# A hybrid layer on one Trainium2 core: the first gate and up unit of the second shared product is issued among the expert tiles

## What is computed

```python
x = x + attn_a(layernorm(x))     # a state-space block, 8 groups of 16 heads, with a convolution in front
x = x + ffn(layernorm(x))        # mixture of experts
x = x + layernorm(x) @ (weight * block_mask).T
x = x + ffn(layernorm(x))        # the same mixture of experts, the same weights

def ffn(x2):                     # 1024 tokens, 512 wide
    shared = (silu(x2 @ Sg.T) * (x2 @ Su.T)) @ Sd.T           # 512 hidden columns, every token
    top2   = the two largest of softmax(x2 @ gate_w.T), scaled to a sum of 1     # 16 experts
    moe    = sum over the two experts e of weight_e * (silu(x2 @ G_e.T) * (x2 @ U_e.T)) @ D_e   # 128 hidden columns
    return moe + shared
```

## Time and profile before

| | us |
|---|---|
| median of 3 runs | 2001.85 |
| lowest and highest of them | 2001.73, 2005.4 |
| the profiled execution: its own time | 1995.66 |
| its span, first to last instruction | 1993.9 |
| PE busy in the span | 1960.6 |
| DVE busy | 1467.4 |
| ACT busy | 1191.9 |
| POOL busy | 1032.7 |

### The profile page before, as it was taken

The page is one execution under the profiler, slowest core; times in us unless marked ns, Lnnn a source line. Parts: engine busy times, 40 slices in busy tenths (PEclk is TensorE's granted clock), DMA queues, the critical chain, the costliest instruction groups (busy, mean ns, idle before and its releaser), DMA issues.

```text
span 1993.9 us, 38125 instructions
## 1 busy us (share of the span) xinstructions
PE 1960.6 (98%) x11776; PEld 1632.7 (82%) x11776; DVE 1467.4 (74%) x2764; ACT 1191.9 (60%) x2602; POOL 1032.7 (52%) x907
## 2 busy tenths in 40 slices
PE   5999999999999999999999999999999999999999
PEld 4888888888888888888888888888888878877887
DVE  8998499849975997599759966996698673167315
ACT  4795388538853884388448744974496444534442
POOL 1596059616951694179417932792289315440433
PEclk8999999999999999999999999999999999999999
DMA  3552145114511351234123413341243139951996
GB/s 107 168 168 58 42 121 168 57 40 124 163 53 57 120 155 48 73 111 152 44 88 109 140 44 93 113 131 43 92 130 113 54 107 327 378 156 48 313 386 198
DMA packets 143909, 253.92 MB, mean 127 GB/s; under 512 B 21448, under 2 KB 37832, under 8 KB 143696
## 3 DMA queue, kind: packets, MB, share of 16 engines
q1 hardware_dynamic: 134848, 231.35, 36.8%
q0 software_dynamic: 7520, 16.80, 2.8%
q10 hardware_dynamic: 1328, 3.15, 0.4%
HBM read 233.38 MB, written 25.69 MB: 130 GB/s over the span
## 4 chain that ended last, share of the span: by engine, by line
PE 91%; DVE 5%; issue 2%; ACT 1%; DMA 1%; DVEq 0%; ACTq 0%; SPq 0%; POOL 0%; POOLq 0%
PE bank L1683 61%; PE bank L1802 7%; PE bank L1992 6%; PE bank L1816 6%; PE bank L1756 4%; PE bank L2004 3%; PE bank L1784 2%; DVE Y L1283 1%; PE bank L1979 1%; PE bank L1691 1%; DVE spare L1380 1%; PE bank L1775 1%; PE bank L1823 1%; DVE Y L1292 1%; DMA cv<-xn_dram,toks 0%
## 5 line engine op out<-in xcount | busy, mean ns | idle before, releaser
L1683 PE MATMUL bank<-xh,wh 128*128 128x512 f32 x1288 | 523.9, 407 | 7.4 <-POOL wl L720 4.0
L1683 PE MATMUL bank<-xh,wl 128*128 128x512 f32 x1288 | 504.9, 392 | 0.0
L1683 PE MATMUL bank<-xl,wh 128*128 128x512 f32 x1288 | 502.8, 390 | 0.0
L720 POOL TENSOR_TENSOR wl<-raw,wh 128x512 fp32r<-128x512 f32 x144 | 192.8, 1344 | 456.7 <-ACT wh L870 456.7
L1283 DVE SCALAR_TENSOR_TENSOR Y<-bank,cpar,Y 128x511 f32<-128x511 f32 (+2 forms) x384 | 286.8, 747 | 23.3 <-ACT Y L914 13.9
L1683 PEld LDWEIGHTS bank<-xh,wh 128*128 128x128 f32 x1288 | 243.0, 189 | 57.2 <-POOL wl L720 4.9
L1683 PEld LDWEIGHTS bank<-xh,wl 128*128 128x128 f32 x1288 | 242.3, 188 | 54.4
L1683 PEld LDWEIGHTS bank<-xl,wh 128*128 128x128 f32 x1288 | 243.4, 189 | 45.8 <-issue 0.5
L737 POOL TENSOR_TENSOR Y<-Y,gt 128x512 f32<-128x512 f32 x128 | 184.1, 1439 | 94.5 <-DVE gt L1337 92.7
L1345 DVE TENSOR_TENSOR al<-Y,ah 128x512 fp32r<-128x512 f32 x128 | 95.8, 749 | 184.3 <-ACT ah L972 184.3
L1683 PE MATMUL bank<-wh,ah 128*128 128x512 f32 x544 | 213.6, 393 | 0.5
(11 more groups left out here) (231 smaller groups left out, 4028.2 us busy)
## 6 DMA issues: line engine op xcount, KB each, us to landing
mem<-c_rows SPq DMA_DIRECT2D x128, 256.0 KB, 3.9
mem<-wffn_d SPq DMA_DIRECT2D x62, 512.0 KB, 6.2
E<-e_rows SPq DMA_DIRECT2D x256, 96.0 KB, 3.5
raw<-wconv_d SPq DMA_DIRECT2D x80, 256.0 KB, 3.0
cv<-c_rows SPq DMA_DIRECT2D x64, 256.0 KB, 4.0
spare<-c_rows SPq DMA_DIRECT2D x64, 256.0 KB, 4.1
raw<-wgate_d SPq DMA_DIRECT2D x64, 256.0 KB, 2.7
raw<-wout_d SPq DMA_DIRECT2D x64, 256.0 KB, 2.7
```

What stands on the lines that cost most here:

```text
L720: inc(pool.tensor_tensor(wl[:, W_SLOT[p], :], raw[:, R_SLOT[p], :], wh[:, W_SLOT[p], :], ALU.subtract), w_lo)
L1683: got = mm(out, l, r, start=first and n == 0, stop=last and n == 2)
```

## The change

In both runs the gate and up matmuls of unit 0 of the second shared product are issued behind the down product of tile 15, in iteration k = 16 of PE's tile loop, ahead of gate and up of tile 17. They go to the banks 4 and 7 in place of 0 and 2. ACT takes the tanh at its k = 16 and makes the high part at k = 17; DVE multiplies behind the hidden rows of tile 16 and makes the low part behind those of tile 17. No work is added or taken out. PE waits for the first shared product's last down add (and in run 0 for the mask, which used bank 4) in place of the end of the tiles.

```diff
+        GU0_AT = 16
+
+        def ffn_banks(i, j):
+            return (4, 7) if i % 2 and j == 0 else (j % 2, 2 + j % 2)
...
-                inc(nc.scalar.activation(gt[:, j % 2, :], bank[j % 2][:, :], ACT.Tanh, scale=0.5), f_th)
+                inc(nc.scalar.activation(gt[:, j % 2, :], bank[ffn_banks(i, j)[0]][:, :], ACT.Tanh, scale=0.5), f_th)
...
                     if 20 <= k <= 21:
                         w_part(second, k - 16)
-                for j in range(4):
+                    if k == GU0_AT:
+                        hidden_tanh(second, 0)
+                    if k == GU0_AT + 1:
+                        hidden_hi(second, 0)
+                for j in range(1, 4):
                     hidden_tanh(second, j)
                     hidden_hi(second, j)
...
-                    inc(STT(gt[:, j % 2, :], gt[:, j % 2, :], 1.0, bank[j % 2][:, :], ALU.add,
+                    inc(STT(gt[:, j % 2, :], gt[:, j % 2, :], 1.0, bank[ffn_banks(i, j)[0]][:, :], ALU.add,
                             ALU.mult), f_hg)
...
-                    inc(TTn(gt[:, j % 2, :], gt[:, j % 2, :], bank[2 + j % 2][:, :], ALU.mult), f_h)
+                    inc(TTn(gt[:, j % 2, :], gt[:, j % 2, :], bank[ffn_banks(i, j)[1]][:, :], ALU.mult), f_h)
...
                 for tau in range(TILES):
                     t_hidden(tau)
+                    if tau == GU0_AT:
+                        hidden_gate(second, 0)
+                        hidden_up(second, 0)
+                    if tau == GU0_AT + 1:
+                        hidden_lo(second, 0)
...
-                hidden(second, 0)
                 combine(0)
                 hidden(second, 1)
...
-                    base, name = ((0, g_mm), (2, u_mm))[n]
+                    name = (g_mm, u_mm)[n]
                     if b == 0:
                         now(pe, f_lo, i, 3 * a + n + 1)
-                    if j >= 2:
+                    if i % 2 and j == 0:
+                        now(pe, dn_acc, i - 1, TT)
+                        if run == 0:
+                            pe.wait_ge(mask_on, 1)
+                    elif j >= 2:
                         now(pe, f_h, i, j - 1)
                     elif i % 2:
                         pe.wait_ge(tx_ok, job(run, TILES))
...
-                        last = three(bank[base + j % 2][:, :], xh[:, kt, b * SEQ:(b + 1) * SEQ],
+                        last = three(bank[ffn_banks(i, j)[n]][:, :], xh[:, kt, b * SEQ:(b + 1) * SEQ],
...
                     if k:
                         t_down(k - 1)
+                    if k == GU0_AT:
+                        gate_up(second, 0, 0, 0)
+                        gate_up(second, 0, 0, 1)
...
-                for what, a, b in FFN_ORDER:
+                for what, a, b in FFN_ORDER[1:]:
```

## The result

The changed kernel takes 2006.76 us (median of 20 runs, 2003.91 to 2009.4) against 2003.06 us (20 runs) for the kernel before beside it: a ratio of 1.0019, with a 95% interval of 1.0013 to 1.0026. That is 3.7 us slower, where 7.2 was forecast. Its own profiled execution took 2004.34 us, with a span of 2002.6, and stands 8.7 us over the profiled execution of before. The two profiles differ by more than twice the medians; most of this study is about why. The profiled execution of before, at 1995.66 us, also lies under all 20 runs of its kernel here, of which the lowest is 1999.43.

A forecast was written before the change was run, and what follows sets the result against it. PE, with 91% of the last chain, was taken to bound the tile loop, and gathers and DVE the tail behind it. Run 0's +3.8 and run 1's +3.4 gave +7.2 us on 2001.85: 2009.0 us, range 2005 to 2014.5.

The forecast's parts named there:

- within 0.2%: Outcome class for the whole kernel: time within 0.2% (4 us) of the kernel before, chance 0.11.
- The move on PE: Tile loop: the unit's 24 matmuls put off the loop's end and first gather by 5.45 us in each run.
- Restarts: PE's changes between tile and shared matmuls in the loop: 0.15 us a run, at most 0.24 each, twice a run.
- What the pause gives back: Tiles behind k = 16: late down weights catch up during the unit, returning 1.5 us in run 0, 1.4 in run 1.
- a unit that is free in the loop: Tile loop: with transfers at 374 GB/s near the 435 GB/s ceiling, the unit would cost nothing; the sum kept 5.45 us.
- The tail of run 0: Behind run 0's loop: DVE's string moves with the loop's end, less its 0.34 us wait for PE; entered as -0.3 us.
- The tail of run 1: Behind run 1's loop: DVE ends 32.7 us behind the loop instead of 33.5, so 0.8 us come back.
- New waits of PE: Tail of run 0: PE waits 1.7 us before unit 3 and 0.9 before down 1, both covered by 3 us.
- The tail follows PE: Rival on both tails: PE sets their end, so the move cancels and relief remains: -2.6 us, 1999.2; chance 0.06.
- the loop follows the transfers: Rival on the tile loop: weights set its pace, the unit is hidden, only tails gain: -1.1 us, 2000.7; chance 0.05.
- No relief: Rival on the tile loop: late tiles stay late, or a new PE wait counts: +10.1 us, 2012.0; chance 0.25.
- the one on the base: Whole kernel: the profiled execution lies 6.2 us under the median of 2001.85, taken as the base for 2009.0.

The follow-up runs named there:

- c_before: The kernel before, unchanged, run again on the first chip: 1995.42 us, ratio 1.0.
- c_after: The changed kernel, unchanged, run again on the first chip: 2003.91 us, ratio 1.0046 to the kernel before.
- h_late: The kernel before with five POOL instructions put ahead of each tail's first gather, third chip: 2007.88 us, ratio 1.0014.
- n_after: The changed kernel without the 16 gathers and the combines of each tail, second chip: 1993.2 us, ratio 0.9933 to the kernel before.
- d_before: The kernel before, unchanged, run again on the third chip: 2005.48 us, ratio 0.9998.
- d_after: The changed kernel, unchanged, run again on the third chip: 2008.23 us, ratio 1.0017 to the kernel before.
- f_spread: The kernel before with the two weight loads of iteration 16 moved to 12 and 20, their splits to 18 and 26: 2022.65 us, ratio 1.0084.
- n_before: The kernel before without the 16 gathers and the combines of each tail, second chip: 1994.84 us, ratio 0.9948 to the kernel before.
- g_early: The kernel before with the first of the two weight loads issued at iteration 9 instead of 16: 2004.39 us, ratio 0.9997.
- s_before: The kernel before with the two weight loads at iteration 16 cut to 16 of 512 columns: 2005.57 us, ratio 0.9994.

## Why the prediction was right, and which term was mis-sized

The direction and the range held, the range with some luck. 2006.76 us lies under the 2008.0 that the terms alone give as their lowest; it is inside because 3 us were added for the spread of the runs. The difference of 3.7 us lies outside the forecast's own 6.2 to 8.5, and at 0.19% it fell on the side of "within 0.2%", which had a chance of 0.11 (the interval reaches to 0.26%). On the first chip the sum can be held against c_before and c_after directly.

**The move on PE** (forecast 5.45 us a run): 5.48 measured. **Restarts** (0.15): none seen. **What the pause gives back** (1.5 and 1.4): the loops grew by 3.97 and 3.87 us, which looks like 1.5 and 1.6. In run 0 that is right: c_before loses 1.6 us behind tile 15 and c_after 0.1. In run 1 it is luck: c_before loses 0.1 us behind tile 15 and 1.4 ahead of it, where the unit can't help, and c_after happens to lose nothing there. This is the term that was mis-sized. Over the twelve loops of the six profiles with the unit behind the tiles, the loss behind tile 15 is 0.1 to 2.4 us and 1.0 on average; with the unit at 16 it is 0.0 to 0.1. So the pause gives back about 1.0 us a run and not 1.5. The prediction took it from one profile, and it had read only run 0's first sixteen iterations, which lose nothing in its window, while those of run 1 lose 1.4 us in the same profile. The cause was named too narrowly as well: the two loads at SP's iteration 16 make tile 19 late, but the loops lose about as much elsewhere with them shrunk or moved.

The Trainium skill (Perfetto Trace Analysis, section Roofline) says that the 16 DMA engines bound a single core at about 435 GB/s. The 374 GB/s of the earlier trace rows stay under it. The consequence that the prediction drew from it, a unit that is free in the loop, didn't come: the unit cost the loops 3.9 us of its 5.5.

**The tail of run 0** (-0.3): -0.1 between c_before and c_after. **The tail of run 1** (-0.8): -0.8. **New waits of PE**: in run 0 1.7 us ahead of unit 3 and 0.9 ahead of down 1 were forecast, and 1.74 and 1.40 came (1.29 and 1.26 in c_after); for run 1 none was named, and 1.16 and 0.86 came. They were covered, as forecast, but by less than the 3 us given: PE waits 1.8 us for the first normed row. The prediction had also read its start wrongly. The earlier trace rows is the second set of transposes; the first is

```profile
1786.35 1.09 PE L1691 MATMUL bank<-ident,cv 128*128 128x128 f32 x8 [0.16 <-DVE cv L1189]
```

so in the kernel before PE and DVE end this tail 0.16 us apart, and not 0.81. These terms make 7.6 us of c_after's 7.7 us in span, but 0.7 us of it comes from ahead of the first loop, where the change does nothing, and the 1.4 us of run 1's early tiles count the other way. With 1.0 us of relief a run the sum would be 11.0 - 2.0 - 0.9 = 8.1 us (an estimate from these profiles) against 8.9 measured by the medians; the forecast was 7.2. Counted from the loop's end, the first gather of run 0 starts 4.2 to 4.7 us behind it in the four profiles of a moved unit with gathers, against 3.6 without the move (h_late aside) and in every run 1; I hadn't foreseen this, and no run isolates its cause.

**Rivals.** "The tail follows PE" and "the loop follows the transfers" would have had c_after at or below c_before; it is 8.9 us above. "No relief" gave +10.1, and the loops show relief; but 8.9 lies between it and the forecast. n_after shows the first rival's mechanism where its condition is made true.

**The step that was off most** is the one on the base: "it lies 6.2 us under the median of 2001.85, which I take as the base". I put the distance between the profiled execution and the median down as a constant that both kernels carry. It isn't one. The kernel before is 11.2 us longer in span on the third chip than on the first (2004.5 against 1993.3), and 11.0 of that is its two tails: 5.9 and 5.1 us. The changed kernel is 4.3 us longer, 1.9 of it in the tails and 2.3 in the loop of run 1, whose early tiles lose 2.2 us more. So the forecast's +7.2 stands on a chip like the one whose profile was read (+8.9 measured), and on the others the kernel before loses in its tails most of what it had ahead. The chip of the first comparison wasn't profiled for the kernel before beside its 20 runs; that it is of the second kind is argued, not shown. For it speak its medians, 2003.06 and 2006.76, and a mark in the profiles: in the first profile of before and in all four of the first chip the profile gives the time to landing of the down weights, 5.1 to 5.6 us (5.4 in the earlier trace rows); in the eight of the other two chips, and in that of the changed kernel beside the 20 runs, it gives none. d_before's row:

```profile
mem<-wffn_d SPq DMA_DIRECT2D x42, 256.0 KB
```

Each chip was used in one session only, so chip and session aren't parted either.

Why the changed kernel loses less is shown as far as this: the waits without a releaser fall from 18.2 us to 1.2. That its tails run one unit fewer, as I expected for d_after, isn't the reason by itself: h_late runs all four units beside its gathers, only with the gathers 4.5 us later, and has 4.3 us of such waits. It may be where the gathers stand against units 2 and 3; no run tests that. No kernel here with the whole computation in it beat the kernel before by more than its interval.

## What to carry to other kernels

Before work is moved off a busy tail, ask what starts at the end of the stage that it moves into: here each 5.5 us unit ahead of the last tile put off sixteen gathers by as much, less about 1 us of late tiles, and the idle time that it left behind was time in which the tail waited anyway. A profiled execution some microseconds under the median is a warning that what stretches the others isn't in the rows; find it before its absence is priced. And before a load or a split is moved along a queue, read what is queued behind its waits, as f_spread shows with 5 us a run. A term of 1 or 2 us needs several profiles: the loops of one program differ by that much.

## What the runs showed that I had not expected

The same program takes 1995 us on one chip and 2005 to 2007 on two others, at a granted clock of 0.995 to 0.996 on both kinds (d_before, c_before), and the difference is in two stretches of about 40 us. In them the results of the gate and up matmuls reach ACT and DVE late, after 1.5 to 5.7 us of idle time each for units 2 and 3, while POOL's indirect gathers run. Without the gathers (n_before, second chip) the tails are 30.1 and 33.4 us and no such wait is there. In d_before the last gather is issued by 1987.2 and the late tanh starts at 1989.11; in run 0 they are at 1778.4 and 1780.36. g_early (run 0), s_before and f_spread (run 1) have the same late tanh, and in all five it starts 1.5 to 2.0 us behind the end of the last gather's instruction.

The signal is late and not the matmuls. PE in d_before, tail of run 1:

```profile
1983.90 0.39 PE L1683 MATMUL bank<-xh,wl 128*128 128x512 f32 x1
1984.13 0.39 PE L1683 MATMUL bank<-wh,ah 128*128 128x512 f32 x1
...
1986.91 0.40 PE L1683 MATMUL bank<-wl,ah 128*128 128x512 f32 x1 [0.35 <-issue]
1987.63 0.48 PE L1683 MATMUL bank<-wh,al 128*128 128x512 f32 x1 [0.32 <-issue]
1988.34 0.39 PE L1683 MATMUL bank<-wh,ah 128*128 128x512 f32 x1 [0.22 <-issue]
1989.05 0.49 PE L1683 MATMUL bank<-wl,ah 128*128 128x512 f32 x1 [0.32 <-issue]
```

The first row is the last up matmul of unit 3, the second the first matmul of down 0. The gate matmuls stand ahead of the 12 up matmuls, so the tanh that starts at 1989.11 had its input complete 7 us earlier. PE itself then halts between single matmuls, for 1.2 us in these rows and 2.4 us in run 0, until the late tanh starts. The profile of this chip also fails to name the releaser of many ordinary waits (22 of ACT and DVE behind 1590 us stand as "issue" in d_before, none in c_before), so "remote" there tells less than the idle time beside it. What holds the signal, and why on some chips only, no run here shows; it stays open.
